# Eight more quads of table rows fetched row by row from ACT's DMA queue in a graph kernel

## The reference

```python
h = jnp.maximum(_layernorm(x, axis=-1), 0.0)
# inside the layer, node_input = h, a = node_vec1
hid = jax.nn.relu(edge_length_embedded @ W_fc1 * (1.0 / np.sqrt(N_BASIS))) * RELU_GAIN
w = hid @ W_fc2 * (1.0 / np.sqrt(N_RADIAL))
w0, w1, w2, w3 = (w[:, :64], w[:, 64:128], w[:, 128:160], w[:, 160:192])
l0, l1 = _fctp_scalar_attr(x0, x1, a, W_l1_0, W_l1_1)
y0 = l0[edge_src]
y1 = l1[edge_src]
m0 = w0 * y0 * e0
m1 = (w1 * y0)[:, :, None] * e1[:, None, :]
m2 = (w2 * e0)[:, :, None] * y1
m3 = w3 * jnp.einsum('eud,ed->eu', y1, e1) * INV_SQRT3
# each m is segment_sum over edge_dst, then the l2 maps; x + out is returned
```

## Time and profile before

| | us |
|---|---|
| median of three runs | 4031.98 |
| span of the profiled execution | 4036.8 |
| POOL busy, indirect DMAs of the main part | 2952.8 |
| PE busy | 3468.5 |
| DVE busy | 2059.2 |
| ACT busy | 1089.5 |

### The profile page before, as it was taken

One profiled execution on the slowest core, in us unless ns is written; L12 is line 12 of the kernel. 1 busy time (PEld: TensorE's weight loads), 2 busy tenths in 40 slices (PEclk: granted clock), 3 DMA queues, 4 the chain that ended last, 5 costly groups with the idle time before them and its releaser, 6 DMA issues.

```text
span 4036.8 us, 67469 instructions
## 1 busy us (share of the span) xinstructions
PE 3468.5 (86%) x17464; PEld 2022.3 (50%) x17464; DVE 2059.2 (51%) x7424; ACT 1089.5 (27%) x2487; POOL 3034.7 (75%) x3203
## 2 busy tenths in 40 slices
PE   5788888888888888888888888888888898888888
PEld 4455445445444545555555545554455454555444
DVE  7454545455445545555455454555455554545554
ACT  5222222222222222222222222222222222222222
POOL 6777777777777777777777777777777777777776
PEclk8788878788778878787887787878788887878887
DMA  9455555555555555555555555555555555555554
GB/s 315 141 148 139 137 142 136 144 143 136 136 139 142 138 142 137 140 138 145 136 144 136 141 134 143 139 140 141 138 143 137 144 137 144 136 142 134 143 145 124
DMA packets 725181, 581.64 MB, mean 144 GB/s; under 512 B 393834, under 2 KB 648126, under 8 KB 724414
## 3 DMA queue, kind: packets, MB, share of 16 engines
q1 hardware_dynamic: 568800, 308.24, 28.3%
q0 software_dynamic: 153552, 262.31, 26.6%
q10 hardware_dynamic: 2446, 6.71, 0.4%
HBM read 421.86 MB, written 155.04 MB: 143 GB/s over the span
## 4 chain that ended last, share of the span: by engine, by line
POOL 38%; DMA 25%; issue 15%; DVE 11%; PE 11%; ACT 0%; DVEq 0%; SPq 0%; POOLq 0%; ACTq 0%
POOL R L819 37%; DMA R<-l_table,src 24%; DVE R L1028 6%; DVE R L1025 4%; PE bank L1105 3%; PE bank L639 3%; PE bank L1118 2%; PE bank L1095 2%; POOL ZD L260 1%; DMA raw_rows<-ZD 0%; PE bank L662 0%; DMA x<-in_xp 0%; DVE R L1014 0%; PE bank L682 0%; DVE st L279 0%
## 5 line engine op out<-in xcount | busy, mean ns | idle before, releaser
L819 POOL DMA_INDIRECT R<-l_table,src x3115 | 2952.8, 948 | 950.2 <-issue 772.4
L1025 DVE TENSOR_TENSOR R<-bank,R 128x256 f32<-128x256 f32 x1600 | 676.9, 423 | 1889.1 <-DMA R<-l_table,src 1288.1
L1105 PE MATMUL bank<-w,hs 100*128 100x192 f32 x6446 | 1536.0, 388 | 88.4 <-DVE R L1028 86.7
L1105 PEld LDWEIGHTS bank<-w,hs 100*128 100x128 f32 x6446 | 1285.6, 228 | 493.4 <-issue 483.4
L1118 PE MATMUL bank<-R 128*32 128x320 f32 x6448 | 740.6, 536 | 419.2 <-DVE R L1028 417.4
L1028 DVE TENSOR_TENSOR R<-bank,R 128x192 f32<-128x192 f32 x3200 | 978.0, 347 | 0.0
L931 ACT ACTIVATE E<-bank 128x320 f32<-128x320 f32 x806 | 352.7, 438 | 2177.3 <-PE bank L1118 2133.0
L1095 PE MATMUL bank<-ea,w1s 10*100 10x512 f32 x1612 | 561.4, 779 | 10.3 <-DMA ea<-in_ea_p 9.5
L925 ACT ACTIVATE hs<-bank 100x512 f32<-100x512 f32 x806 | 437.5, 594 | 393.1 <-PE bank L1095 393.1
L1118 PEld LDWEIGHTS bank<-R 128*32 128x32 f32 x6448 | 149.7, 117 | 659.8 <-issue 658.6
L639 PE MATMUL bank<-ZD 128*128 128x448 f32 x776 | 393.8, 660 | 0.0
(11 more groups left out here) (109 smaller groups left out, 829.3 us busy)
## 6 DMA issues: line engine op xcount, KB each, us to landing
s_tiles<-E SPq DMA_DIRECT2D x806, 160.0 KB
R<-l_table,src POOLq DMA_INDIRECT x3115
ea<-in_ea_p SPq DMA_DIRECT2D x403, 96.0 KB
ZD<-s_tiles SPq DMA_DIRECT2D x392, 96.0 KB, 2.5
ZD<-s_tiles SPq DMA_DIRECT2D x97, 320.0 KB
psc<-l_table SPq DMA_DIRECT2D x1536, 0.6 KB
H<-l_table SPq DMA_DIRECT2D x1536, 0.6 KB
ZD<-s_tiles SPq DMA_DIRECT2D x391, 48.0 KB, 3.1
```

Source lines behind the costliest of these rows:

```text
L819: PL.indirect_dma_start(out=Y[:, g % NB, t, :], out_offset=None, in_=T, in_offset=bass.IndirectOffsetOnAxis(ap=src[:, k:k + 1], axis=0),). ...
L1025: V.tensor_tensor(p[:, :, :, 0:64], w[:, :, 0:128].rearrange("p t (s c) -> p t s c", s=2), y[:, :, 0:64].unsqueeze(2).to_broadcast([128, n ...
L1105: m = PE.matmul(b[:, o * 192:(o + 1) * 192], hs[:, g % 4, t * 128:(t + 1) * 128], w2[:, :], start=True, stop=True, skip_group_check=True)
```

## The change

Eight further quads (82, 157, 264, 372, 446, 562, 668, 742) leave POOL's list. ACT issues one plain DMA of 640 bytes for each of their 512 rows, from row numbers that it loads RA = 16 at a time from a new input table. The issues stand at the end of ACT's turn. The rows of quad h are spread evenly from four turns before the previous such quad (from turn 2 for the first) to five turns before h: 6.7 and 6.8 rows per turn for quads 82 and 157, 6.9 for 446 and 742, 4.8, 4.7, 4.4 and 4.8 for the other four. Two new landing buffers of one quad each, `lone_act`, are used in turn; the third and later of these quads wait until DVE has used the quad two before. DVE reads its operand from `lone_act` for these quads, after a wait for all 512 rows. SP's row quads now also wait once for all 512 rows, where they had one semaphore for each half. The prologue gets one more DMA on ACT's queue, for the row numbers.

```diff
+NACT = 8
+RA = 16
+def single_act(n_nodes, n_edges):
+    nt, ng = plan(n_nodes, n_edges)
+    raw = [g for k, g in raws(n_nodes, n_edges)]
+    taken = set(raw) | set(single(n_nodes, n_edges))
+    n = min(NACT, len(raw))
+    some = [raw[(2 * i + 1) * len(raw) // (2 * n)] + 9 for i in range(n)] if n else []
+    return [g for g in some if g < ng - 1 and g not in taken]
...
+        src_act = sb("src_act", [128, max(NRA, 1), RA], i32)
+        lone_act = sb("lone_act", [128, 2, G, C])
...
                 AC.dma_start(src_row[:, :, :], a["src_row"]).then_inc(s_si, 16)
+                AC.dma_start(src_act[:, :, :], a["src_act"]).then_inc(s_sa, 16)
...
             for g in range(NG):
-                if g in raw_of or g in row_of:
+                if g in raw_of or g in row_of or g in rowa_of:
                     continue
...
-                    SP.dma_start(lone[i % 2][n:n + 1, t, :], T[bass.ds(v, 1), :]).then_inc(s_rw[i][t // 2], 16)
+                    SP.dma_start(lone[i % 2][n:n + 1, t, :], T[bass.ds(v, 1), :]).then_inc(s_rw[i], 16)
...
+            def act_row(i, n):
+                if n == 0:
+                    if i == 0:
+                        AC.wait_ge(s_sa, 16)
+                        for c in range(3):
+                            AC.wait_ge(s_T[c], 16 * ((NQ + 2 - c) // 3))
+                    if i >= 2:
+                        AC.wait_ge(s_p, 2 * ROWA[i - 2] + 2)
+                if n % RA == 0:
+                    c, p = divmod((i * GE + n) // RA, 128)
+                    held[:] = [AC.alloc_register(f"arow{i}_{n}_{k}") for k in range(RA)]
+                    AC.load(held, src_act[p:p + 1, c, :])
+                t, p = divmod(n, 128)
+                v = bass.RuntimeValue.of_register_unchecked(held[n % RA]).with_bounds(min_val=0, max_val=NP - 1)
+                AC.dma_start(lone_act[p:p + 1, i % 2, t, :], T[bass.ds(v, 1), :]).then_inc(s_rwa[i], 16)
+                AC.free_register(held[n % RA])
+            def act_rows(g):
+                for i, h in enumerate(ROWA):
+                    lo, hi = (ROWA[i - 1] - 4 if i else 2), h - 4
+                    if lo <= g < hi:
+                        for n in range((g - lo) * GE // (hi - lo), (g + 1 - lo) * GE // (hi - lo)):
+                            act_row(i, n)
...
                 for r in raw_at(g, 3):
                     raw_rear(r)
+                act_rows(g)
...
                     elif g in row_of:
-                        V.wait_ge(s_rw[row_of[g]][u], 16 * 256)
+                        V.wait_ge(s_rw[row_of[g]], 16 * GE)
+                    elif g in rowa_of:
+                        V.wait_ge(s_rwa[rowa_of[g]], 16 * GE)
```

More of the change, by code:

```diff
@@ L89, in build @@
     NRC = -(-len(ROW) * (GE // RB) // 128)
+    ROWA = single_act(n_nodes, n_edges)
+    rowa_of = {g: i for i, g in enumerate(ROWA)}
+    NRA = -(-len(ROWA) * (GE // RA) // 128)
     NRB = 7
@@ L212, in build @@
         s_si = sem("s_si")
+        s_sa = sem("s_sa")
         s_rg = [sem(f"s_rg{b}") for b in range(NRB)]
@@ L784, in build @@
             s_rp = sem("s_rp")
-            s_rw = [[sem(f"s_rw{i}_{u}") for u in range(2)] for i in range(len(ROW))]
+            s_rw = [sem(f"s_rw{i}") for i in range(len(ROW))]
+            s_rwa = [sem(f"s_rwa{i}") for i in range(len(ROWA))]
             lone = [psc[:, :, :].rearrange("p q c -> p (q c)")[:, 0:G * C].rearrange("p (t c) -> p t c", t=G),
@@ L802, in fetched @@
                 return 16 * sum(len(tiles(h, u)) for h in range(g % NB, g + 1, NB)
-                                if h not in raw_of and h not in row_of)
+                                if h not in raw_of and h not in row_of and h not in rowa_of)
             def raw_at(g, d):
@@ L971, in raw_rear @@
                 AC.activation(y[:, 3, :], bank[7][:, 96:256], ACT.Copy, scale=rar[:, 3:4]).then_inc(s_ro, 1)
+            held = []
+            def act_row(i, n):
[20 more added lines that the diff above has]
+                            act_row(i, n)
             for g in range(4):
@@ L1021, in weigh @@
                 w = three[slot(g, u)][:, 0:192 * nt].rearrange("p (t c) -> p t c", t=nt)
-                from_ = lone[row_of[g] % 2] if g in row_of else Y[:, g % NB, :, :]
+                if g in row_of:
+                    from_ = lone[row_of[g] % 2]
+                elif g in rowa_of:
+                    from_ = lone_act[:, rowa_of[g] % 2, :, :]
+                else:
+                    from_ = Y[:, g % NB, :, :]
                 y = from_[:, 2 * u:2 * u + nt, :]
@@ L1377, in lay_out @@
         src_row[i * GE // RB:(i + 1) * GE // RB] = src[g * GE:(g + 1) * GE].reshape(-1, RB)
+    ROWA = single_act(n_nodes, n_edges)
+    src_act = np.zeros((-(-max(len(ROWA) * GE, 1) // (128 * RA)) * 128, RA), np.int32)
+    for i, g in enumerate(ROWA):
+        src_act[i * GE // RA:(i + 1) * GE // RA] = src[g * GE:(g + 1) * GE].reshape(-1, RA)
     far = np.full(len(tile) + SPAN, -(1 << 20), np.int32)
@@ L1382, in lay_out @@
     return {
+        "src_act": np.ascontiguousarray(src_act.reshape(-1, 128, RA).transpose(1, 0, 2)),
         "src_row": np.ascontiguousarray(src_row.reshape(-1, 128, RB).transpose(1, 0, 2)), "xp": xp, "xa": np.concatenate([xp, avec], axis=1), "src_raw": np.ascontiguousarray(src_raw.T), "avec": np.ascontiguousarray(avec.reshape(NT, 128).T), "src_t": np.ascontiguousarray(src.reshape(-1, 128).T),
```

## The result

The changed kernel takes 3994.37 us, the median of four runs (3991.67 to 3994.78), against 4031.68 us (4031.2 to 4032.61) for the kernel before: ratio 0.9906, 95% interval 0.9893 to 0.9919. It is 37.3 us faster, where 40.1 were forecast, at 3991.9 us. The profiled execution has a span of 3990.3 us and a run time of 3994.23, so 4 us of a run lie outside the span.

A forecast was written before the change was run, and what follows sets the result against it. POOL's unbroken line of fetches was taken as the bound: median 4031.98 less 40.1 us for 32 fetches, with no cost on POOL, ACT or small parts, gives 3991.9 us; range 3989 to 4012 for eight in ten.

The forecast's parts named there:

- The bound and the gain: POOL's gapless line of fetches sets the end; eight quads of four fetches fewer save 32 x 1.253 = 40.1 us.
- The cadence: POOL's time per fetch, 1.253 us, stays unchanged under more DMA traffic; outer bounds -0.2% and +0.3%.
- The tail: The last 18 us after POOL's line stay, since 61 fetched quads follow the last skipped one.
- ACT's row: One row issue on ACT, taken from SP's rows: 0.43 us, 6.9 per heavy turn, 2.97 us.
- ACT's load: A load of 16 row numbers on ACT: 0.6 us without growth by count, 0.26 us per turn.
- The upper bound of the step: ACT's load growing with its count: 4 x 0.507 = 2.03 us, 0.87 per turn.
- ACT's need: ACT's rows, loads and present work in a heavy turn: 4.51 us, fitting within POOL's about 4.8 us.
- Lateness: ACT's rows delay its next copy by some 0.6, up to 3 us; short PE stalls are free while POOL's lead covers them.
- the 15.6 of the earlier trace: POOL's time in hand, in us, between DVE's finishing with a ring half and POOL's reuse, after a DVE stall.
- Rival 2: ACT keeps its waits for PE, 0.87 us per turn; need 5.38 us, total 4118 us; chance 0.07.
- Rival 1: Load grows with count, nothing of ACT overlaps: 5.12 us per turn, 4041 us; mild form chance 0.12, strong forms 0.06.
- Rival 3: Rows take no effective load off POOL: full ring after skipped quads or stretched cadence; at most no change, 4032 us; no-change chance 0.05.

The follow-up runs named there:

- waits_only: Kernel before plus 34 already satisfied semaphore waits in each of ACT's turns 2 to 737, no DMA: 5272.35 us against 5170.35, ratio 1.0193.
- no_sp_rows: Kernel before without SP's six row quads, which POOL fetches instead: 5115.48 us against 5170.35, ratio 0.9892.
- ra4: Changed kernel with four row numbers per load on ACT instead of 16: 5431.82 us, ratio 1.0370 to the kernel before.

## Why the prediction was right, point by point

- **The bound and the gain.** Forecast: 32 fetches off a line without gaps, 40.1 us. The trace after has the line that the earlier trace rows show of before: 3083 fetches and no wait over 0.3 us. This, and no experiment, is the evidence that ACT's rows were hidden: whatever ACT lost would have had to reach POOL as a longer wait for DVE, and there are none.
- **The cadence.** Taken as unchanged. Between the two profiled executions it fell by 0.22%, but worked out from the median run of before it is 1.250 us in both. The last fetch starts at 3969.2 us and not at the forecast 3978.4 for this reason. The prediction took its 4.8 us from the profiled execution to the median run as the difference of a span and a run time; that cost nothing, since the forecast is the median less 40.1. More row traffic didn't stretch it: ACT's queue moved 9.37 MB at 0.8% of the DMA engines' time.
- **The tail.** Forecast: 18 us, unchanged. It took 21.1, for the half clock in the profiled execution. The mechanism and the order of work were right; this term is the one that was mis-sized, by 2.8 us, and it is nearly all that parts the measured 37.3 from the forecast 40.1. The prediction gave the clock no term at all.
- **ACT's row.** 0.43 us forecast from SP's four in a row, 0.39 measured between neighbours.
- **ACT's load.** 0.6 us forecast, "four cost no more than one, so I take no growth"; 1.33 measured. This step failed. The single number on ACT (0.637) and the four on SP (0.507) are on different engines, in different parts of the program, and no line held a load of 16. The upper bound of the step (2.03) held it. The prediction named "a load of 16 above 1.3 us" as a sign of being wrong: it was seen, and the time was still right.
- **Why that didn't matter.** ACT's need in a heavy turn becomes 6.9 x 0.39 + 0.43 x 1.33 + 1.28 = 4.54 us, against the forecast 4.51: the cheaper row pays for the dearer load. That the two errors cancel is luck; with the forecast row and the measured load the sum is 4.82. A turn took 4.71 to 4.82 us in the four heavy stretches, by the starts of L951.
- **Lateness.** "Some 0.6 us, and up to 3 us late", with PE's waits for ACT between 7.7 and 100 us: the copies show it (3.1 us at 408.43, 4.6 at the worst, 32 of them over 3), and PE's waits for hidden values rise from 7.7 to 33.8 us. POOL's smallest time in hand, from the end of DVE's last use of a half of the ring to the fetch that overwrites it, is 13.9 us after and 14.4 before, both worked out from the traces' starts; the 15.6 of the earlier trace rows was not the smallest. All of ACT's lateness was absorbed there.
- **Rivals.** Rival 2 (ACT keeps its waits for PE) is half borne out: the radial wait shrank from 393.1 to 272.4 us, while the closing wait rose, from 305.3 to 334.5, so 606.9 us of its 698.4 stayed. They did not add to ACT's need all the same, or POOL would have waited. Rival 1's growth with the count is real, but 0.06 us per number and not 0.13, so with the row of 0.39 its sum is 4.54 even with nothing overlapped. Rival 3 (POOL gains nothing) is ruled out by the cadence of 1.250 us and waits of 0.3 us at most. The estimate by the Trainium skill, "Runtime: NRT & Kernel Launch", section "Instruction fetch mechanics" (200 ns per register, 3.2 us for 16), is refuted by 1.33 us, 83 ns per register. The floor of about 600 ns that the Trainium skill gives in "DMA: Bandwidth & Descriptors", section "Latency and other measured facts", fits ACT's 0.593 us for four and not its 1.33 us for 16; SP's medians for four, 0.507 and 0.540 us, lie under it.
- **What the prediction did not see.** It took the issuing queues' speed as given. Where the kernel before takes 5239 us, POOL's line is no longer the bound, and the change turns from 0.9% faster to 3.2% slower. That POOL has slack there and that instructions on ACT and SP are paid for is shown by POOL's waits, waits_only and no_sp_rows. What makes the kernel 1140 to 1210 us longer there is open: SP's steps stretch (4 rows in up to 7 us), but without them it is as slow within 55 us, and since the unchanged kernel has it as well, the change did not make it.

## What to carry to other kernels

When an engine's line has no gap from the first link to the last, count its links: the gain is their number times the cadence, and the other engines need only be checked for having time in hand, per turn and in the heaviest stretch. Price a new instruction from a row of the same size or take both ends; a load of more numbers is a larger load. A gain of this kind holds only where that line is the bound: the same change gained 37 us where POOL never waited and lost 169 us where it waited over 1000. So look at the waits of the saturated engine in the conditions in which the kernel will run, before taking a gain of 1% for granted.

## What the runs showed of the hardware

- A load of row numbers into registers took 0.593 us for four (ra4) and 1.330 us for 16 (the changed kernel) on ACT, and 0.507 and 0.540 us for four on SP, in the two traces near 4000 us; all are medians.
- One-row DMA issues from a register followed each other at 0.39 us on ACT, with 0.235 us of that the issue itself.
- 18 of the last multiplications of 128x160 took 4.90 us in the trace whose clock was granted at half and 2.88 us in the one at full, 2.0 us less.
- Waits on satisfied semaphores are not free everywhere: where the kernel before takes 5170 us, 12512 of them on ACT cost 102 us, 8 ns each in the mean.
- In that condition a fetch still takes POOL 0.946 us and SP's queue needs the same time of the DMA engines (1134 us against 1142), while single register operations on SP take up to 1.409 us instead of 0.047.
